# New orders of the engines' steady step in a decoder kernel, with six changes of PE tile shape a step, the self output inverted ahead of the self maxima, and another front of the drain

## The reference, cut to what matters

```python
# x: (64, 64, 128), ctx: (64, 64, 128), 16 heads of 8
x = x + self_attention(layernorm(x))      # one projection Wv serves as q, k and v; then Wo
x = x + cross_attention(layernorm(x), ctx, ctx)   # no projections
h = layernorm(x)                          # then a top-1 mixture of 7 experts + a shared one
x = x + 0.5 / w * swiglu(h, shared) + p / w * swiglu(h, expert[argmax])
# self_attention: p = x @ Wv.T + bv; softmax(p p^T / sqrt(8)) p, per head; out @ Wo.T + bo
```

## Time and profile before

| | |
|---|---|
| time, median of 3 runs | 427.58 us (427.24 to 427.79) |
| span of the profiled execution | 427.0 us |
| PE busy | 404.4 us, 95% |
| DVE busy | 305.1 us, 71% |
| ACT busy | 298.5 us, 70% |
| POOL busy | 284.8 us, 67% |
| steps 5 to 32 of the pipeline | 32.75 to 233.79 us |

### The profile page before, as it was taken

The page is one execution under the profiler, slowest core; times in us unless marked ns, Lnnn a source line. Parts: engine busy times, 40 slices in busy tenths (PEclk is TensorE's granted clock), DMA queues, the critical chain, the costliest instruction groups (busy, mean ns, idle before and its releaser), DMA issues.

```text
span 427.0 us, 16199 instructions
## 1 busy us (share of the span) xinstructions
PE 404.4 (95%) x5545; PEld 312.9 (73%) x5546; DVE 305.1 (71%) x791; ACT 298.5 (70%) x684; POOL 284.8 (67%) x476
## 2 busy tenths in 40 slices
PE   7989999999998999999999898969999999999997
PEld 4646666666665666666665667959988999999996
DVE  7868999999998998999999787713333444444444
ACT  7659999999998999999998685302213466666651
POOL 8757788878887888888888423665664463444442
PEclk9999999999999999999999999996999999999999
DMA  6254566767676667765444300021113255430001
GB/s 104 43 85 64 87 103 108 109 110 121 120 124 117 114 123 126 143 101 84 60 63 43 35 2 2 27 81 58 69 69 90 67 133 139 131 104 27 27 32 52
DMA packets 176324, 35.22 MB, mean 82 GB/s; under 512 B 145587, under 2 KB 174646, under 8 KB 176256
## 3 DMA queue, kind: packets, MB, share of 16 engines
q1 hardware_dynamic: 71296, 21.43, 23.1%
q10 hardware_dynamic: 102144, 6.81, 15.2%
q0 software_dynamic: 2816, 6.10, 4.1%
HBM read 20.86 MB, written 15.67 MB: 86 GB/s over the span
## 4 chain that ended last, share of the span: by engine, by line
PE 68%; DMA 10%; issue 6%; DVE 6%; ACT 3%; SPq 2%; POOL 2%; another core or an unknown queue 2%; DVEq 0%; ACTq 0%; POOLq 0%
PE psum L867 15%; PE psum L659 12%; PE psum L668 12%; PE psum L973 8%; PE psum L680 7%; DMA orow<-attention_out 3%; DMA attention_out<-on_s 3%; PE psum L690 3%; SPq L198 2%; DMA ring<-sorted_rows 2%; PE psum L763 2%; PE psum L802 2%; PE psum L758 1%; PE psum L809 1%
## 5 line engine op out<-in xcount | busy, mean ns | idle before, releaser
L1583 DVE TENSOR_TENSOR gT<-gT,psum 128x384 f32<-128x384 f32 x66 | 36.5, 553 | 77.5 <-PE psum L867 34.4
L1263 ACT ACTIVATE gT<-psum 128x384 f32<-128x384 f32 x70 | 33.6, 488 | 58.4 <-PE psum L867 36.9
L620 POOL DMA_INDIRECT out<-yrow,token x38 | 37.1, 975 | 41.2 <-DVE yrow L1718 22.0
L973 PE MATMUL psum<-wdn_sb,gT 128*128 (+1 forms) x420 | 60.2, 280 | 4.0 <-DVE rows_all L1597 2.2
L479 POOL TENSOR_TENSOR k_s<-pT,hmask_sb 128x1024 f32<-128x1024 f32 x32 | 61.0, 1906 | 0.9 <-ACT pT L1137 0.8
L973 PEld LDWEIGHTS psum<-wdn_sb,gT 128*128 128x128 f32 x420 | 53.3, 195 | 5.7 <-issue 2.7
L867 PE MATMUL psum<-fhT,wtile 128*128 128x128 f32 x456 | 57.2, 275 | 0.3 <-ACT wtile L1292 0.3
L867 PE MATMUL psum<-hT_all,wup_sb 128*128 128x128 f32 x384 | 50.9, 283 | 5.0 <-issue 3.8
L867 PEld LDWEIGHTS psum<-fhT,wtile 128*128 128x128 f32 x456 | 53.9, 192 | 0.5 <-ACT wtile L1292 0.5
L867 PEld LDWEIGHTS psum<-hT_all,wup_sb 128*128 128x128 f32 x384 | 47.7, 198 | 6.0 <-issue 4.8
L1065 ACT ACTIVATE pr_x<-pr_x,rs 128x512 f32<-128x512 f32 x60 | 43.0, 722 | 8.2 <-DVE pr_x L1368 7.0
(11 more groups left out here) (193 smaller groups left out, 872.0 us busy)
## 6 DMA issues: line engine op xcount, KB each, us to landing
sorted_rows<-nowhere_row SPq DMA_DIRECT2D x38, 130.0 KB, 3.6
ring<-sorted_rows SPq DMA_DIRECT2D x30, 130.0 KB
wup_sb<-in_wup SPq DMA_DIRECT2D x14, 176.0 KB, 3.0
orow<-attention_out SPq DMA_DIRECT2D x31, 64.0 KB
ring<-in_ctxv ACTq DMA_DIRECT2D x60, 32.0 KB, 3.7
cross_keys<-in_ctxk ACTq DMA_DIRECT2D x14, 128.0 KB, 3.7
ring<-cross_keys SPq DMA_DIRECT2D x112, 16.0 KB
rows_all<-in_x ACTq DMA_DIRECT2D x10, 128.0 KB, 3.9
```

The lines of the kernel that those rows point to most:

```text
L620: pool.indirect_dma_start(out=out, out_offset=bass.IndirectOffsetOnAxis(ap=token[p][:, 0:1], axis=0), in_=yrow[p][:, :], in_offset=None, b ...
L973: last = nc.tensor.matmul(ps_y[p], gT[place_of(n) if isinstance(n, int) and n < FIRST else p][:, c, :], wdn_sb[:, expert, c, :], start=(c ...
```

## The change

The first five steps (`STEADY = LAG["pv_x"]`, 5) keep the old orders, in functions named `opening`. From step 5 on:

- **PE**: the row's turn_output, which stood at the end of a body, stands at the head of the next one. Then turn s of both groups, turn_back x, project, weigh s, scores s, turn x of group 0, the new row, turn x of group 1, turn_back s, query, weigh x of group 0, the two projections, weigh x of group 1, scores x. The shape changes six times a step, where it changed seven times.
- **DVE**: normalise x, invert s, normalise s, mean_variance s, maxima s, soften s twice, moments x, moments p, mean_variance x, mean_variance p, maxima x and soften x group by group (four instructions in the place of two), the sum, invert x, moments s.
- **ACT**: keys, second store, both exponentials s, the x eviction, the output, both turned s, and the values only behind them (they stood behind the keys). The copy of the new row stands between the two cross copies.
- **POOL**: the masked keys stand first in the body; the added bias and the added cross attention stand behind the centred query and its variance.
- **Drain**: turn_output of unit 29, the first turned rows, turn_back x and project come ahead of the turns of unit 31, with ACT to match; DVE inverts unit 30 ahead of the maxima of unit 31.
- **Opening**: two more matmuls that keep the clock, at step 3.

The diff, cut to the orders themselves:

```diff
@@ POOL
             def body(t, u, live):
                 i = t % 2
+                steady = t >= STEADY
                 pool.wait_ge(sem("mv_set"), 2)
+                if live("proj") and steady:
+                    keys_masked(u["proj"])
...
+                if live("xb") and steady:
+                    bias_added(u["xb"])
+                if live("on_x"):
+                    cross_added(u["on_x"])
@@ PE
+                if t < STEADY - 1:
+                    keep_clock((1, 4, 4, 2)[t], bank[3])
...
+            def body(t, u, live):
+                if t < STEADY:
+                    return opening(t, u, live)
+                if live("q"):
+                    turn_output(u["q"])
+                if live("soft_s"):
+                    turn("s", u["soft_s"], 0)
+                    turn("s", u["soft_s"], 1)
+                if live("on_x"):
+                    turn_back("x", u["on_x"])
+                if live("q"):
+                    project(u["q"])
+                if live("soft_s"):
+                    self_weighed(u["soft_s"])
+                if live("S_s"):
+                    self_scores(u["S_s"])
+                turn("x", u["pv_x"], 0)
+                if live("xT"):
+                    new_row(u["xT"])
+                turn("x", u["pv_x"], 1)
+                if live("soft_s"):
+                    turn_back("s", u["soft_s"])
+                if live("q"):
+                    query(u["q"])
+                cross_weighed(u["pv_x"], (0,))
+                if live("xT"):
+                    self_projected(u["xT"])
+                cross_weighed(u["pv_x"], (1,))
+                if live("q"):
+                    cross_scores(u["q"])
...
-            turn("s", U - 1, 0)
-            turn("s", U - 1, 1)
+            turn_output(U - 3)
             pe.wait_ge(sem("p_v"), U)
             pe.wait_ge(sem("p_pT"), U)
             turn_rows(0)
+            turn_back("x", U - 5)
             pe.wait_ge(sem("s_onT"), at(U - 3))
             project(U - 3)
+            turn("s", U - 1, 0)
+            turn("s", U - 1, 1)
@@ ACT
+                if live("proj"):
+                    keys_out(u["proj"])
+                if live("out"):
+                    second_store(u["out"])
+                if live("soft_s"):
+                    exp("s", u["soft_s"], 0)
+                    exp("s", u["soft_s"], 1)
+                if live("on_x"):
+                    evicted("x", u["on_x"])
+                if live("q"):
+                    output(u["q"])
+                if live("soft_s"):
+                    turned("s", u["soft_s"], 0)
+                    turned("s", u["soft_s"], 1)
+                if live("proj"):
+                    values_out(u["proj"])
@@ DVE
+            def body(t, u, live):
+                if t < STEADY:
+                    return opening(t, u, live)
+                if live("st_x"):
+                    normalise("x", u["st_x"])
+                if live("out"):
+                    invert("s", u["out"])
+                    normalise("s", u["out"])
+                mean_variance("s", u["pv_x"] + LAG["q"], u["pv_x"])
+                if live("soft_s"):
+                    maxima("s", u["soft_s"])
+                    soften("s", u["soft_s"], 0)
+                    soften("s", u["soft_s"], 1)
+                if live("st_x"):
+                    dve.wait_ge(sem("x_x"), at(u["st_x"]))
+                    moments("x", u["st_x"])
+                if live("norm"):
+                    first_moments(u["norm"])
+                if live("st_x"):
+                    mean_variance("x", t, u["st_x"])
+                if live("norm"):
+                    mean_variance("p", t, u["norm"])
+                maximum_of("x", u["pv_x"], 0)
+                maximum_of("x", u["pv_x"], 1)
+                soften("x", u["pv_x"], 0)
+                soften("x", u["pv_x"], 1)
+                if live("q"):
+                    attention_added(u["q"])
+                if live("on_x"):
+                    invert("x", u["on_x"])
+                if live("q"):
+                    query_moments(u["q"])
...
-            moments_x(U - 6)
-            maxima("s", U - 1)
             invert("s", U - 2)
             normalise("s", U - 2)
+            maxima("s", U - 1)
+            moments_x(U - 6)
```

More of the change, by code:

```diff
@@ L763, in project, with new_row, self_weighed, self_scores @@
                 nc.tensor.matmul(ps_wo, onT[:], wo_sb[:], start=True, stop=True).then_inc(sem("s_wo"), 1)
-            def body(t, u, live):
+            def new_row(u):
+                pe.wait_ge(sem("p_xn"), at(u))
+                if u >= 1:
+                    pe.wait_ge(sem("p_v"), u)
+                    pe.wait_ge(sem("p_pT"), u)
+                nc.tensor.transpose(ps_xT, xn["p"][:], id_sb[:]).then_inc(sem("p_xT"), 1)
+            def self_weighed(u):
+                pe.wait_ge(sem("p_v"), at(u))
+                weigh("s", u, 0, v_s[u % 2][:])
+                weigh("s", u, 1, v_s[u % 2][:])
+            def self_scores(u):
+                pe.wait_ge(sem("s_khd"), at(u))
+                scores("s", u, pT, k_s)
+            def self_projected(u):
+                pe.wait_ge(sem("p_xnT"), at(u))
+                for b in range(NB):
+                    for j in range(4):
+                        h2, k = j // 2, S * b + VW * (j % 2)
+                        last = nc.tensor.matmul(
+                            ps_v[VW * j:VW * (j + 1), S * b:S * (b + 1)], xnT[:, k:k + VW],
+                            wv_sb[:].rearrange("p (a c d) -> p c a d", a=HP, c=2)[:, h2, :, :], start=True, stop=True,
+                            tile_position=(0, VW * j))
+                last.then_inc(sem("p_pv"), 1)
+                for j in range(4):
+                    rows = slice(VW * j, VW * (j + 1))
+                    last = nc.tensor.matmul(ps_pT[rows, :], wv_sb[:, rows], xnT[:], start=True, stop=True, tile_position=(0, VW * j))
+                last.then_inc(sem("p_p"), 1)
+            def opening(t, u, live):
                 if live("soft_s"):
@@ L1128, in output, with keys_out @@
                 nc.scalar.copy(onT[:], ps_oT).then_inc(sem("s_onT"), 1)
-            def body(t, u, live):
-                if live("proj"):
[L1132 to L1142, removed]
-                        last = nc.scalar.copy(v_s[u["proj"] % 2][rows, :].rearrange("p (a b e) -> p b a e", a=HP, b=NB)[:, :, :, DK * h2:DK * (h2 + 1)],
-                                              ps_v[rows, :].rearrange("p (b a d) -> p b a d", a=HP, b=NB))
-                    last.then_inc(sem("p_v"), 1)
+            def keys_out(u):
+                act.wait_ge(sem("p_p"), at(u))
+                act.wait_ge(sem("p_pv"), at(u))
+                if u >= 1:
+                    act.wait_ge(sem("s_khd"), u)
+                    act.wait_ge(sem("s_sc"), u)
+                nc.scalar.activation(pT[:], ps_pT, ACT.Identity, bias=bv_sb[:, 0:1]).then_inc(sem("p_pT"), 1)
@@ new lines, in values_out @@
+            def values_out(u):
+                if u >= 2:
+                    act.wait_ge(sem("s_pv"), G * (u - 1))
+                act.wait_ge(sem("p_pv"), at(u))
+                for h2 in range(2):
+                    rows = slice(S * h2, S * (h2 + 1))
+                    last = nc.scalar.copy(v_s[u % 2][rows, :].rearrange("p (a b e) -> p b a e", a=HP, b=NB)[:, :, :, DK * h2:DK * (h2 + 1)],
+                                          ps_v[rows, :].rearrange("p (b a d) -> p b a d", a=HP, b=NB))
+                last.then_inc(sem("p_v"), 1)
```

184 lines of the change are left out of this document (80 added, 104 removed).

## The result

| | before | after |
|---|---|---|
| time, median | 427.69 us (427.24 to 428.45, 4 runs) | 472.57 us (470.72 to 473.62, 4 runs) |
| span of the profiled execution | 427.0 us | 469.6 us |
| one ordinary step | 7.05 us | 8.74 us |
| steps 5 to 32 | 201.0 us | 243.2 us |

A forecast was written before the change was run, and what follows sets the result against it. PE's stream was taken to bound the kernel before, a new query chain the changed one: 427.0 + 41.7 = 468.7 us profiled, 0.6 below the median, so 469 us; range 456 to 484.

The forecast's parts named there:

- The chain of the query: Turn_back s, inversion, normalise, mean_variance, centring, query: 1.91 us where it was 0.22, so 1.7 us of PE idle each step.
- The rest of the step: Turn s 4.45 us after turn_back s, then 4.07 to about 4.4 to the next turn_back s: step 8.7 us.
- second store: Its issue, now ahead of the self exponentials, holds ACT's queue 0.63 us before turn s.
- Late rows: Rows back late from memory stall PE; they should go, their 3.6 us lying within the 201.0 replaced.
- The sum: Steps 4 to 32 together 242.7 us against 201.0: +41.7 us, with drain and opening at zero.
- body 4: Last body of the opening, filler matmuls between turn_back and query: a stall of 0.8 us.
- my bound: The drain's change in time, taken as zero, with -1 to +2 us.
- the first: Rival: only the self softmax binds, turn s 3.7 us after turn_back s; step 7.8 to 8.1, 449 us; 8%.
- The second: Rival: the inversion costs no wait and the change of shape decides; faster, 421 to 424 us; 5%.
- The clock rival: PE's clock falls to its lower level for a fifth of the pipeline: some +38 us, 507 and more; 6%.
- a gap of 1.35 us: PE's idle time ahead of a late row, with the step behind it at its usual pace; so no clock term.
- change of shape: Weigh x of group 1 beside neighbours of its shape saves PE 0.12 us a step, 3.4 over 28 steps.

The follow-up runs named there:

- experiment 1: The changed kernel with mean_variance s moved back ahead of invert s and normalise s on DVE: 450.44 us, 1.0537 times the kernel before.
- experiment 4: The kernel before with only invert s and normalise s moved ahead of mean_variance s and maxima s, from step 5 on: 471.97 us, ratio 1.1017.
- experiment 3: The changed kernel with mean_variance s and maxima s ahead of invert s, and ACT's second store behind the two self exponentials: 422.51 us, ratio 0.9892.
- experiment 2: The changed kernel with mean_variance s and maxima s ahead of invert s and normalise s on DVE: 425.72 us, ratio 0.9962.
- experiment 8: The changed kernel with moments p moved between normalise s and mean_variance s on DVE, no work added: 484.48 us, ratio 1.1235.
- Experiment 5: The kernel before with weigh x of group 1 ahead of scores x on PE: 430.90 us, ratio 1.0078.
- experiment 6: The kernel before with maxima and subtraction of the cross scores group by group on DVE: 426.34 us, ratio 0.9956.
- its repeat: The changed kernel with moments p ahead of mean_variance s, run again on another chip: 475.27 us; with three filler matmuls ahead of the query 464.08 us.
- the last three kernels: The changed kernel with moments p ahead of mean_variance s: with three filler matmuls 463.90 us; run again without them 475.27, with them 464.08 us.

## Why the prediction was right, and where it was not

*The chain of the query.* Right, term by term. Turn_back to inversion 0.42 (0.42 forecast), to normalise 0.29 (0.28), to the mean 0.21 (0.21), to POOL 0.27 (0.29), to the query 0.66 (0.61 and 0.10): 1.85 us for 1.91. The only term that no row showed, the signal from POOL to PE, is 0.05, at the low end of its bounds. Experiments 1 and 4 show that it is the cause.

*The rest of the step.* Turn s starts 4.40 us after turn_back (117.58, one step ahead of 126.32, to 121.98), forecast 4.45, and turn_back 4.34 after turn s, forecast between 4.07 and 4.4. The step of 8.74 was forecast as 8.7. The second store holds ACT's queue as the prediction had it, and in the changed kernel it all but hides behind the pause: turn s starts 0.24 us behind turn_output, 0.17 in experiment 3. Its full price showed itself only in experiments 2 and 3. Late rows went, as forecast: no turn_output waits for its row in the list of waits of the steady steps.

*The sum.* Turn_output of step 5 starts at 34.17 where the old one stood at 32.75: +1.4 for the opening, in which I had 0.8 for body 4 and zero for two matmuls that keep the clock. Of the 1.4, 1.1 stand already at the turn_output of step 3 (27.09 for 25.99), which in the profiles of kernels with this opening lies anywhere from 26.1 to 27.1 and so says little. From the turn_output of step 3 to that of step 4 the changed kernel takes 7.08 us, the kernel before 6.76, and that of experiment 2, with the changed kernel's opening, 6.25: the stall of body 4 is 0.8, as forecast, and the opening without it is half a microsecond shorter than the old one, for which I had no term. The 28 steps to the first instruction of the drain take 243.2 us, +42.2. What follows is 192.2 us where it was 193.2, so the new drain gives 1.0, the low end of my bound; it may be the earlier inversion or the new front, no run took them apart. Together +42.6 for the 41.7 of the sum, so that errors of 1.9 and -1.0 partly cancel.

*The median.* The largest error of size is in the plainest term: the 0.6 us between the span of the trace before and the median. The profiled run of the changed kernel took 471.82 us around a span of 469.6, 2.2 us more, and the median is 0.8 above that. Of the 3.6 us between 469 and 472.57, 2.4 are this, 0.9 the sum and 0.3 rounding.

*The rivals.* The price of the first (449) was that of experiment 1 (450.4): it is the chain next in line. The second's (421 to 424) was that of experiment 3 (422.5), though not of 2. The clock rival did not come: 1.00 in all of the pipeline. The gap of 1.47 us in each step, which the prediction named as a risk, did not bring it about. But I gave it 6% on the grounds that a gap of 1.35 us was harmless, and 0.19 us on top of the 1.47 that the change made was enough (experiment 8). It was nearer than 6% says.

*What bounds the kernel before.* Here the reading failed. "In an ordinary step PE never rests" is what the records show, and I took PE's stream to bound the step, with 0.2 us of waits as a trifle. Experiment 5 took a change of shape off that stream and the kernel got 3.0 us slower; experiment 6 left the stream alone and it got 1.6 us faster. The bound was the loop of the cross softmax, whose length is the step, while the turns, with their waits for ACT between matmuls, soaked up the difference. The change of shape itself is worth a little more on PE than I said, 0.16 us for 0.12, but in the kernel before, PE spends the gain waiting, and the 3.4 us of the step are not there. That was luck: it cost the forecast nothing only because the new chain is longer than these loops. The 0.15 us that DVE waited for scores should have led me to add up such loops.

## What to carry to other kernels

In a software pipeline of engines that each take their work in order, a step is as long as the longest loop from an instruction through the other engines back to itself a step later; add these loops up before reading busy shares, for a busy engine can be the one that waits. When an instruction that waits is moved ahead, everything behind it on its engine waits for the same thing, and what counts is who needs those: here 0.17 us of work was needed by the very instruction that stood next behind the one waited for. A short instruction whose input has long been ready belongs ahead of one that waits.

## What was not expected of the hardware

- A pause of 1.47 us in each step of 8.74 left the granted clock at 1.00; with one of 1.66, some steps stayed at 8.93 us and 1.00 and others took 10.3 us at a mean clock of 0.83, in experiment 8 and in its repeat. Filler that does nothing useful made the repeat's kernel 11.2 us faster.
- Chips differ by 3% on the kernel before: 428 us, and 414 to 416 us beside the last three kernels. A ratio is only good beside runs of the same chip.
- The issue of one store from ACT's queue (0.62 us) ahead of an exponential whose input was ready cost 3.2 us over 28 steps, 7.05 for 6.94 us each (experiments 2 and 3, on two chips with the kernel before at the same 428 us).
